# Loading the last batch's x1 and th in two parts (chunks 0 to 5, then chunk 6), with the row of ones written by GpSimd

## The reference, cut to what matters

```python
# x: (8, 96, 64, 64), seen as 8 batches x 96 channels x 4096 tokens
x = x + mamba(group_norm(x))        # in_proj, 4-tap conv, selective scan over the tokens with 16 states,
                                    # gate by silu(z), out_proj, layer norm over the channels
t = to_tokens(x)                    # this is x1
n = ln_t(t)                         # this is th (normalised tokens)
q, k, v = split(n @ Wqkv + bqkv)    # 6 heads of 16
t = t + (q @ k.T * 16**-0.5) @ v @ Wff + bff     # no softmax: per batch one 97x96 matrix applied to th
t = t + q_acc(W2 q_mul(relu(q_acc(W1 q_mul(ln_t(t)) + b1))) + b2)    # fp8 (5,2) products, f16 sums
```

## Time and profile before

| what | value |
|---|---|
| median of 3 runs | 2520.53 us (2520.23 to 2521.58) |
| profiled execution: its own time | 2531.32 us |
| profiled execution: span of the core | 2529.5 us |
| mean granted TensorE clock | 0.963 |
| busy share: VectorE, GpSimd, ScalarE, TensorE | 97%, 95%, 92%, 84% |
| mean DMA traffic over the span | 195 GB/s |

### The profile page before, as it was taken

The page is one execution under the profiler, slowest core; times in us unless marked ns, Lnnn a source line. Parts: engine busy times, 40 slices in busy tenths (PEclk is TensorE's granted clock), DMA queues, the critical chain, the costliest instruction groups (busy, mean ns, idle before and its releaser), DMA issues.

```text
span 2529.5 us, 34487 instructions
## 1 busy us (share of the span) xinstructions
PE 2129.8 (84%) x10022; PEld 790.6 (31%) x10022; DVE 2458.5 (97%) x2390; ACT 2316.7 (92%) x3960; POOL 2414.4 (95%) x718
## 2 busy tenths in 40 slices
PE   6787888888888888888888888888888888888877
PEld 3223323233333333323333323323323333333323
DVE  7999999999999999999999999999999999999986
ACT  5677777999999999999999999999999999999977
POOL 4999999999999999999999999999999999999981
PEclk8788878999999999999999999999999999999979
DMA  6555554555665665665656656656565566566533
GB/s 241 188 184 162 198 177 161 201 203 198 211 211 189 218 212 184 216 210 191 219 199 198 215 196 205 208 202 210 198 210 210 195 212 202 183 215 206 174 123 85
DMA packets 171162, 494.51 MB, mean 195 GB/s; under 512 B 23040, under 2 KB 44672, under 8 KB 154016
## 3 DMA queue, kind: packets, MB, share of 16 engines
q1 hardware_dynamic: 170976, 492.30, 57.8%
HBM read 400.33 MB, written 91.88 MB: 195 GB/s over the span
## 4 chain that ended last, share of the span: by engine, by line
DVE 69%; issue 11%; POOL 8%; PE 7%; ACT 4%; DMA 1%; DVEq 0%; SPq 0%; POOLq 0%; ACTq 0%
DVE R L1204 52%; DVE D L1188 10%; POOL R L666 6%; PE G L1428 2%; POOL D L645 2%; ACT DA L828 1%; DVE q L1284 1%; DVE G L1229 1%; DVE dl L1214 1%; PE G L1462 1%; DVE yv L1225 1%; PE Y L1505 1%; PE G L1465 1%; DVE th L1237 1%; DMA R<-ths 1%
## 5 line engine op out<-in xcount | busy, mean ns | idle before, releaser
L1204 DVE TENSOR_TENSOR_SCAN R<-DA,R,D 128x512 f32<-128x512 f32 x1344 | 1627.6, 1257 | 4.5 <-ACT DA L828 4.5
L666 POOL TENSOR_TENSOR R<-R,Cs 128x2048 f32<-128x2048 f32 x383 | 1452.7, 3815 | 2.0 <-DVE R L1204 2.0
L828 ACT ACTIVATE DA<-ds,kept_w 128x512 f32<-128x512 f32 x1536 | 1054.4, 688 | 143.4 <-DVE R L1204 129.3
L645 POOL TENSOR_TENSOR D<-us,Bs 128x2048 f32<-128x2048 f32 x193 | 736.7, 3817 | 9.6 <-DMA us<-lo_d 9.4
L1188 DVE TENSOR_TENSOR D<-us,PB 128x2048 f32<-128x2048 f32 x191 | 357.8, 1874 | 6.9 <-DMA us<-lo_d 6.9
L1462 PE MATMUL G<-un,wcv 96*128 96x512 f32 x512 | 262.4, 637 | 29.4 <-ACT h L895 29.4
L1505 PE MATMUL Y<-R,kept_w 128*32 128x512 f32 x2048 | 267.7, 618 | 8.9 <-POOL R L666 8.9
L1204 DVE TENSOR_TENSOR_SCAN R<-DA,D 128x512 f32<-128x512 f32 x192 | 221.8, 1204 | 3.3 <-ACT DA L828 3.3
L1465 PE MATMUL G<-un,wcv 96*64 96x256 f32 x1024 | 148.7, 415 | 60.3 <-ACT xq L876 59.1
L1428 PE MATMUL G<-st,kept_w 128*64 128x256 f32 (+1 forms) x384 | 113.3, 502 | 66.2 <-ACT st L790 66.2
L1428 PE MATMUL G<-sq,kept_w 96*96 96x512 f32 (+1 forms) x256 | 143.7, 645 | 23.9 <-DVE dl L1214 20.9
(11 more groups left out here) (231 smaller groups left out, 3227.6 us busy)
## 6 DMA issues: line engine op xcount, KB each, us to landing
Bs<-bc_d SPq DMA_DIRECT2D x128, 512.0 KB, 5.4
us<-lo_d SPq DMA_DIRECT2D x64, 1024.0 KB, 6.6
ds<-lo_d SPq DMA_DIRECT2D x64, 1024.0 KB, 8.5
Cs<-bc_d SPq DMA_DIRECT2D x128, 512.0 KB, 4.8
us<-hi_d SPq DMA_DIRECT2D x64, 512.0 KB, 6.9
ds<-hi_d SPq DMA_DIRECT2D x64, 512.0 KB, 5.4
lo_d<-dl SPq DMA_DIRECT2D x64, 256.0 KB, 2.0
lo_d<-du SPq DMA_DIRECT2D x64, 256.0 KB, 2.0
```

What stands on the lines that cost most here:

```text
L645: nc.gpsimd.tensor_tensor(shaped(D[:, s % NDBU, :, :], s), low(us, s) if s in LOWS else high(us), of_states(Bs, s), ALU.mult).then_inc(don ...
L666: nc.gpsimd.tensor_tensor(shaped(R[:, s, :, 0:T], s), shaped(R[:, s, :, 1:S], s), of_states(Cs, s), ALU.mult).then_inc(hc_done.sem, 1)
L828: nc.scalar.activation(DA[j % NDA][:, :], ds[:, i, :], ACT.Exp, scale=A[:, j:j + 1]).then_inc(exp_done.sem, 1)
L1204: nc.vector.tensor_tensor_scan(R[:, s, q, 1:S], DA[j % NDA][:, :], D[:, s % NDBU, q, :], before, ALU.mult, ALU.add).then_inc(scanned.sem, 1)
```

## The change

`load_late` becomes `late_part(k, n)`, which loads n chunks from chunk k. Its first call (chunks 56 to 61) stands at the head of SyncE's iteration 64, ahead of `store(51)`; the x1 half waits for quads 0 and 1 of chunk 63 to be summed, the th half for quads 0 to 3. The second call (chunk 62) stands where `load_late` stood. VectorE's wait for all six quads and its memset go; GpSimd does the memset after its last product, once quads 0 to 3 are summed. TensorE asks for both loads of each tensor only from chunk 62 on.

```diff
-            def load_late():
-
-                sp_eng.wait_ge(summed.sem, summed.at(LAST))
-                sp_eng.wait_ge(x1_out, kept(LAST - 1))
-                sp_eng.wait_ge(th_out, kept(LAST - 1))
-                src = slice(0, (CH - 1) * T)
-                sp_eng.dma_start(tx[:, 0:CH - 1, :], x1s[B - 1, :, src].rearrange("c (k t) -> c k t", t=T)).then_inc(late_x, 16)
-                sp_eng.dma_start(tn[0:C, 0:CH - 1, :], ths[B - 1, :, src].rearrange("c (k t) -> c k t", t=T))\
+            def late_part(k, n):
+                src = slice(place(k) * T, place(k + n) * T)
+                at = slice(place(k), place(k + n))
+                sp_eng.wait_ge(x1_out, kept(k + n - 1))
+                sp_eng.wait_ge(th_out, kept(k + n - 1))
+                sp_eng.wait_ge(summed.sem, summed.at(LAST, 2))
+                sp_eng.dma_start(tx[:, at, :], x1s[B - 1, :, src].rearrange("c (k t) -> c k t", t=T)).then_inc(late_x, 16)
+                sp_eng.wait_ge(summed.sem, summed.at(LAST, 4))
+                sp_eng.dma_start(tn[0:C, at, :], ths[B - 1, :, src].rearrange("c (k t) -> c k t", t=T))\
                     .then_inc(late_t, 16)
 
             def iteration(g):
+                if g == LAST + 1:
+                    late_part(LAST + 1 - CH, CH - 2)
                 if there(g) and g > 0:
                     load_c(g, 0)
...
-                    load_late()
+                    late_part(LAST - 1, 1)
...
             iterations(pool, iteration)
+            pool.wait_ge(hc_done.sem, hc_done.at(LAST))
+            pool.wait_ge(summed.sem, summed.at(LAST, 4))
+            nc.gpsimd.memset(tn[C:C + 1, 0:CH - 1, :], 1.0).then_inc(w_ready, 1)
...
-                dve.wait_ge(summed.sem, summed.at(k))
-                nc.vector.memset(tn[C:C + 1, 0:CH - 1, :], 1.0).then_inc(w_ready, 1)
...
-                    pe.wait_ge(late_t, 16)
-                    pe.wait_ge(late_x, 16)
+                    pe.wait_ge(late_t, 32 if m == LAST - 1 else 16)
+                    pe.wait_ge(late_x, 32 if m == LAST - 1 else 16)
```

## The result

The changed kernel takes 2530.45 us (median of 19 runs), the kernel before 2524.27 (19 runs beside it). The ratio is 1.0022, with a 95% interval of 1.0012 to 1.0033: slower by 5.5 us, between 3.0 and 8.3. Single executions of either kernel differ by 10 us and more (before 2519.74 to 2534.84), mostly through the 64 chunks of scans, which the change doesn't touch: in three traces of before the mark named next comes at 2457.52, 2443.02 and 2451.44 us, while all that follows it differs by 2.9 us at most. So the traces are compared from a mark in the ending: the start of VectorE's gate of chunk 63, the `yv` product of 128x512. In the trace shown of before it starts at 2457.52 us, in that of the changed kernel at 2453.11. From the mark to the end of the span is called the **tail** here: 2529.5 - 2457.52 = 71.98 us before, 2532.5 - 2453.11 = 79.39 us after.

A forecast was written before the change was run, and what follows sets the result against it. Scans set the span until about 2457 us, then the ending's serial chain; 6.4 + 1.8 - 0.25 - 0.5 = +7.45 us, so 2520.53 + 7.5 = 2528.0 us, range 2522.5 to 2531.

The forecast's parts named there:

- The early loads' issue: On SyncE's queue, the x1 load goes out at about 2455.0 us and the th load at 2457.6.
- store(51) held: On SyncE's queue, store(51), issued at 2458.0 us, lands only behind both early loads, at 2468.2 us.
- The lower landing of 2466.5 us: Lower estimate of when store(51) lands: near 2466.5 us, with the early loads moving at 235 GB/s.
- last_add_x +6.4 us: In the ending, xq lands at 2472.9 us, so last_add_x starts at 2472.95 instead of 2466.51: +6.4 us.
- The half clock +1.8 us: TensorE, idle about 7 us before centre_tokens(54), restarts with 3.6 us of low clock: +1.8 us, between 0 and 3.5.
- The memset -0.25 us: Without VectorE's memset ahead of last_norm, the ending gains 0.25 us; GpSimd's own memset costs nothing.
- The wait at late_apply(56) -0.5 us: TensorE's 1.54 us wait for the late th load vanishes, but only 0.5 us of it come through.
- rival 2: SyncE's store(51) passes the loads, landing at 2460.2 us: 2519.8 us; partial form +0 to +3 us; chance 0.15 together.
- rival 1: Ending stalls, but TensorE's clock holds or loads drain at 235 GB/s or more: +3.5 to +5.6 us; chance 0.20.
- rival 3: TensorE's clock stays low through the folds up to the pipeline, or the drain takes longer: +9 to +12 us; chance 0.10.

The follow-up runs named there:

- ScalarE's queue: The changed kernel with the six-chunk early loads issued by ScalarE on its own queue, both waiting for quads 0 to 3: ratio to before 1.0015, tail 79.38 us.
- keeping TensorE busy: The changed kernel with 12 extra products of 256 columns, never read, ahead of centre_tokens(54): ratio to before 1.0017, tail 76.98 us.

## Why the prediction came out as it did

The time, 2530.45 us, lies in the range and the sign is as forecast. Step by step, with what was forecast first:

- **The early loads' issue.** 2455.0 and 2457.6 on before's time are 2.5 us ahead of the mark and 0.1 behind it; measured 2.38 ahead and 0.01 ahead. Right.
- **store(51) held.** Landing 10.7 us behind the mark; measured 10.2 and 10.5. Right, and shown by four, six and two chunks and by the store put first. The prediction speaks of a large DMA ahead on this queue. ScalarE's queue shows that it needn't be the same queue: a load issued elsewhere holds the small ones as well. The lower landing of 2466.5 us doesn't follow from the prediction's own terms, which give 2455.0 + 2.1 + 10.0 = 2467.1.
- **last_add_x +6.4 us.** Measured +5.66 and +6.30. Right, a little large: `load_x1(54)` went out at 10.26 and 10.63 us, not 10.73, and in the first trace `xq` landed in 3.4 us, not 3.7 (3.7 in the second).
- **The half clock +1.8 us.** Measured +2.35 and +2.04 (13.48 and 13.17 against 11.13 with the memset moved), and 2.34 by keeping TensorE busy. Right in kind, a little small: by the stretches shown above the low clock ended at about 2472.4 us, 5.1 us after TensorE had begun again at 2467.27, and not 3.6. Of the 2.35 us, 0.76 are `centre_tokens(54)`, which the prediction has adding nothing; at half clock it holds up `last_centre`.
- **The memset -0.25 us.** Measured -0.35 to -0.37 in the six traces that have it on GpSimd and keep the clock through that stretch. GpSimd's own took 3.08 us, beside idle time.
- **The wait at late_apply(56) -0.5 us.** This is the term that was mis-sized. At full clock only 0.24 us come through (51.50 to 51.26), half of what was forecast. But in two of before's three traces the clock fell in that wait, and then it costs 2.2 to 3.1 us; the mean of the three is 53.13, so its removal is worth 1.9 us. The prediction reads one trace, in which the clock held, and applies the rule of the clock to the new idle stretch only, not to the old one.

The sum, +7.45, matches the first pair of traces (+7.41), and that match is luck twice over. The terms' errors cancel (0.7 us too much at `last_add_x`, 0.6 too little for the clock), and the trace of before that was read is its best case; against the mean the change costs 5.9, by the timed runs 5.5. Of the rivals, the store that isn't held (rival 2) is refuted by the landings, the held clock (rival 1) by both traces of the changed kernel, the clock that stays low into the pipeline (rival 3) too: it was back at 2472 to 2474 us. Rival 1's faster drain, to 2466.5 us or 9.0 behind the mark, isn't borne out either (10.2 and 10.5). The timed difference alone wouldn't have told it from the forecast: 5.5 us lies in rival 1's +3.5 to +5.6 and just under the forecast's +5.6 to +9. Of the chances, 0.70 for slower by over 0.2% is 0.73 by the prediction's own terms, since half of rival 1 is 0.10 and rival 3 another 0.10.

The level of 2528.0 us is 2.5 under the median, which lies 0.55 us inside the range's upper end. Two errors work against each other there: the forecast started from 2520.53 us, the median of three runs of before, where the nineteen have 2524.27, 3.7 us more, and it had the change over a microsecond too large. From 2524.27 it would have been 2531.7.

The gain that lies at this place is to be had: with two chunks in the early part, the wait and the fall of the clock in it go, the memset is off VectorE, and the tail is 71.36 us in both runs against a mean of 73.6 before. The medians lean the same way (0.9993 and 0.9987), but their intervals reach 1.0007 and 1.0000, so the gain of the whole kernel is indicated, not established.

## What to carry to other kernels

When a large load is moved forward, list every small DMA that is issued while it drains, on any queue, and give each its deadline: here the late load had 15 us of transfer but only 1.5 us of wait to win, and of the DMAs that it got in front of the tightest had 1.4 us of slack. Split the load so that the part ahead fits that slack; only the first piece has to be early. And in a serial piece with TensorE on it, price an idle stretch with the clock's fall, the old ones as well as the new ones, and from more than one execution.

## What the runs showed of the hardware

- A 192 KB DMA issued 2.5 us or more behind 2304 KB of loads landed 7.9 to 8.5 us after its issue, and 9.7 to 10.1 us when issued 0.4 us behind them, where it takes 2.1 to 3.8 without them. It took 10.4 to 10.5 us when the loads were on the other engine's queue, where both had been issued together at the mark and the second landed after 12.2 us.
- In that run SyncE's queue moved 0.15 MB of its 0.98 by the time at which ScalarE's had moved all of its 2.36 MB.
- An idle stretch of TensorE of 1.54 us left the clock at 2.4 GHz, of 1.67, 2.00, 2.08, 2.11 and 2.15 us it fell to 1.2 GHz. Two traces of one kernel, 0.13 us apart in the wait, lie on both sides; whether the length or chance decides between them, these traces don't show. The Trainium skill ("TensorE: Matmul & The Clock Gate", section "HAM oscillation — how this bites in real kernels") warns of longer gaps than these; here each of these five gaps of 1.67 to 2.15 us was followed by the fall.
- The memset of 3584 elements on one partition takes 3.08 us on GpSimd and 3.04 on VectorE.
